# Values' product of weights as half-precision pairs, split in place among nine tiles of gates, and weight scales summed over partitions by TensorE

## The reference, cut to what matters

```
x = x + 0.5 * ffn(layernorm(x)); x = x + attn(layernorm(x)); x = x + 0.5 * ffn(layernorm(x))
# ffn(x): thought = x_norm[:, -1] @ agg_w, then four steps of thought += gelu(ln(thought) @ d1_w) @ d2_w
#         broadcast = thought @ bc_w;  gate = sigmoid(x @ gate_w);  out = layer_norm(x + gate * broadcast)
# attn(x): windows of 128, scores of own and previous window, squared relu, weighted sum of values
qkv = x @ w_attn.T          # q, k, v
sim = einsum('bwie,bwje->bwij', bq, bk2);  attn = square(relu(sim))
out = einsum('bwij,bwje->bwie', attn, bv2) @ w_o.T
```

## Time and profile before

| | us |
|---|---|
| runs of the kernel before: median (lowest to highest of 3) | 2115.79 (2107.5 to 2125.19) |
| the profiled execution's own time | 2117.86 |
| its span, first to last instruction | 2116.6 |
| PE busy in the span | 2037.7 (96%) |
| DVE / ACT / POOL busy | 1173.0 / 664.7 / 159.0 |
| DMA engines' mean share | 75.5%, 263 GB/s |

### The profile page before, as it was taken

One profiled execution on the slowest core, in us unless ns is written; L12 is line 12 of the kernel. 1 busy time (PEld: TensorE's weight loads), 2 busy tenths in 40 slices (PEclk: granted clock), 3 DMA queues, 4 the chain that ended last, 5 costly groups with the idle time before them and its releaser, 6 DMA issues.

```text
span 2116.6 us, 30247 instructions
## 1 busy us (share of the span) xinstructions
PE 2037.7 (96%) x11872; PEld 1037.0 (49%) x11872; DVE 1173.0 (55%) x2108; ACT 664.7 (31%) x931; POOL 159.0 (8%) x281
## 2 busy tenths in 40 slices
PE   8988989999999999998999999999999999999997
PEld 3333433444333446655665555665556564444443
DVE  2321323554344465567676755655555545888887
ACT  0557322433223232222333221211212113444443
POOL 0000000000000010000000000000000000111111
PEclk9999999999999999999999999999999999999999
DMA  8788897988988833348989799898987947555552
GB/s 340 237 311 341 285 353 269 379 319 320 354 338 333 332 132 118 100 140 299 323 294 327 273 320 293 297 347 283 313 290 278 357 149 221 149 151 154 154 149 80
DMA packets 275213, 555.76 MB, mean 263 GB/s; under 512 B 149040, under 2 KB 149248, under 8 KB 274688
## 3 DMA queue, kind: packets, MB, share of 16 engines
q1 hardware_dynamic: 275072, 553.83, 75.5%
HBM read 406.93 MB, written 113.26 MB: 246 GB/s over the span
## 4 chain that ended last, share of the span: by engine, by line
PE 47%; DMA 3%; DVE 2%; SPq 2%; ACT 1%; issue 1%; POOL 0%; ACTq 0%; DVEq 0%
PE product_banks L1023 41%; PE product_banks L1143 3%; PE thought_acc L1208 3%; DMA thought_units<-parts_scratch 1%; DMA gate_arena<-arena 1%; DMA arena<-in_x 0%; SPq L810 0%; DVE thought_units L1754 0%; SPq L944 0%; DMA thought_units<-in_d_w 0%; ACT arena L1315 0%; PE thought_turn L1216 0%; ACT arena L1318 0%; PE thought_acc L1198 0%; DVE arena L1566 0%
## 5 line engine op out<-in xcount | busy, mean ns | idle before, releaser
L1023 PE MATMUL product_banks<-gate_arena,arena 128*128 128x512 f16 x1536 | 354.1, 382 | 0.0
L1023 PE MATMUL product_banks<-wide_a,thought_units 128*128 128x512 f16 x1536 | 331.7, 379 | 0.0
L1023 PE MATMUL product_banks<-gate_arena,wide_a 128*128 128x256 f16 x2688 | 307.5, 274 | 2.4 <-DMA gate_arena<-arena 2.4
L1023 PE MATMUL product_banks<-wide_b,gate_arena 128*128 128x512 f16 x1344 | 301.8, 380 | 0.0
L1023 PEld LDWEIGHTS product_banks<-gate_arena,wide_a 128*128 128x128 f16 x2688 | 260.4, 98 | 59.5 <-issue 28.9
L1054 PE MATMUL product_banks<-wide_a,wide_b 128*128 128x512 f32 x512 | 240.9, 616 | 7.1 <-DMA wide_a<-in_w_attn 6.3
L1023 PEld LDWEIGHTS product_banks<-gate_arena,arena 128*128 128x128 f16 x1536 | 145.0, 98 | 203.6 <-issue 51.0
L1023 PEld LDWEIGHTS product_banks<-wide_a,thought_units 128*128 128x128 f16 x1536 | 150.3, 98 | 181.6 <-DVE arena L1606 0.5
L1023 PEld LDWEIGHTS product_banks<-wide_b,gate_arena 128*128 128x128 f16 x1344 | 127.2, 98 | 167.5 <-issue 24.9
L1423 DVE BATCH_NORM_STATS2 bn_parts<-arena 128x6 f32<-128x512 f32 x256 | 164.3, 684 | 4.4
L1054 PEld LDWEIGHTS product_banks<-wide_a,wide_b 128*128 128x128 f32 x512 | 95.1, 195 | 137.9 <-issue 137.8
(11 more groups left out here) (168 smaller groups left out, 2090.1 us busy)
## 6 DMA issues: line engine op xcount, KB each, us to landing
thought_units<-parts_scratch SPq DMA_DIRECT2D x268, 512.0 KB, 6.1
thought_units<-in_d_w SPq DMA_DIRECT2D x148, 512.0 KB, 6.7
thought_row<-in_d_w SPq DMA_DIRECT2D x76, 512.0 KB, 7.2
arena<-in_x SPq DMA_DIRECT2D x64, 512.0 KB, 8.8
parts_scratch<-thought_units SPq DMA_DIRECT2D x64, 512.0 KB, 6.2
x_scratch<-arena SPq DMA_DIRECT2D x64, 512.0 KB, 6.8
arena<-x_scratch SPq DMA_DIRECT2D x40, 512.0 KB, 6.0
gate_scratch<-arena SPq DMA_DIRECT2D x32, 512.0 KB, 8.3
```

The lines of the kernel that those rows point to most:

```text
L1023: mm = pe.matmul(bank, left(i, k), right(j, k), start=(n == 0), stop=(n == 3 * KD - 1))
```

## The change

- The fold `vo` becomes three f16 products for each float32 one. wv (in `wide_b`) and the transposed w_o (in `wide_a`) are split in place: the two halves of row block e are written over block e - 1, block 0's into a spare slot. So ACT's high half of block e waits for DVE's low half of e - 1 (`fold_split`). Before that, DVE takes the largest value of each block (`top`, 16 reductions of 128x1024) and two more scales are made (`wv`, `wo`). ACT's copy of the result is scaled by their inverse.
- The scale of a matrix: DVE reduces over the rows (`scale_t`), TensorE multiplies one column by a matrix that holds 1/1024 everywhere (`scale_a`, into a bank of the transposes), DVE multiplies by 1024 (`scale_b`). It is the sum over partitions of their largest values, where GpSimd's was the largest. There are now five scales.
- Nine tiles of gates stand before the fold `vo` (`EARLY` = 9): four with the loads of wv and w_o, five with the tops and splits. 19 tiles stand after it in place of 25, and they take the whole of reading back and splitting, and `gate_save`, which stood among the fold.
- The planner's cost of a `vo` piece goes from 1.83 to 1.28.
- In the first list the norms of the first two tiles stand before their transposes. In the first group of stage 2 the values of tile 0 come before the queries, and only these need the first transposed tile alone.

```diff
-EARLY, LATE = 3, 4
+EARLY, LATE = 9, 4
-        return 1.0 if piece[1:3] == ("qk", 0) else 1.83 * FOLD_SIZES[piece[2]]
+        return 1.0 if piece[1:3] == ("qk", 0) else (1.83 if piece[1] == "qk" else 1.28) * FOLD_SIZES[piece[2]]
...
+            own = [p for p in products if p[0] == "v" and p[2] == 0]
+            products = own + [p for p in products if p not in own]
...
-    early = paced([p for n in range(EARLY) for p in plan_gate(n)], wo, 0.9, PE_PIECES)
-    save = [("gate_save", k) for k in range(KD)] + [("params",)] + [("rest",)] * 6 + [("half_params",)]
-    fold_vo = paced(plan_fold("vo"), save, 0.5, PE_PIECES)
-    fold_vo.append(("fold_store", "vo", KD - 1))
+        if n >= 2:
+            wo.append(("top", "wv", n - 2))
+    wo += [("top", "wv", KD - 2), ("top", "wv", KD - 1), ("scale_t", "wv"), ("rest",), ("scale_a", "wv"), ("rest",),
+           ("scale_b", "wv")]
+    sides = [("top", "wo", e) for e in range(KD)] + [("fold_split", "wv", e) for e in range(2)] + [("scale_t", "wo")]
+    sides += [("fold_split", "wv", 2), ("scale_a", "wo"), ("fold_split", "wv", 3), ("scale_b", "wo")]
+    sides += [("fold_split", "wv", e) for e in range(4, KD)] + [("fold_split", "wo", e) for e in range(KD)]
+    early = paced([p for n in range(4) for p in plan_gate(n)], wo, 1.45, PE_PIECES)
+    early += paced([p for n in range(4, EARLY) for p in plan_gate(n)], sides, 0.75, PE_PIECES)
+    fold_vo = plan_fold("vo") + [("fold_store", "vo", KD - 1)]
...
-    gates = paced([p for n in range(EARLY, TILES - LATE) for p in plan_gate(n)], splits, 0.3, PE_PIECES)
+    gates = paced([p for n in range(EARLY, TILES - LATE) for p in plan_gate(n)], splits, 0.65, PE_PIECES)
...
+                        pe.wait_ge(side_split["wv"], e + 1)
+                        pe.wait_ge(side_split["wo"], e + 1)
...
+                        for n, (i, j) in enumerate(((0, 0), (0, 1), (1, 0))):
+                            mm = pe.matmul(bank_ap(key), fold_parts("wv", e)[:, i, d * P:(d + 1) * P],
+                                           fold_parts("wo", e)[:, j, h * BANK:(h + 1) * BANK], start=(e == n == 0),
+                                           stop=(e == KD - 1 and n == PARTS - 1))
...
+                pe.wait_ge(top_found, SCALE_AT[m] + 1)
+                pe.matmul(turn_ap((kind, m))[:, 0:1], mean_maker[:, :], scale_stat[m][:, KD:KD + 1], start=True,
+                          stop=True).then_inc(turn_full, 1)
...
+            elif kind == "fold_split":
+                m, e = a
+                if e == 0:
+                    act.wait_ge(scale_made, SCALE_AT[m] + 1)
+                else:
+                    act.wait_ge(side_split[m], e)
+                act.activation(fold_parts(m, e)[:, 0], fold_side[m][:, e, :], ACT.Copy,
+                               scale=scale_stat[m][:, KD + 2:KD + 3]).then_inc(side_high[m], 1)
...
+                if m == "wv":
+                    dve.wait_ge(q_piece[k], 32)
...
-                pool.partition_all_reduce(scale_stat[m][:, KD + 1:KD + 2], scale_stat[m][:, KD:KD + 1], P,
-                                          bass.bass_isa.ReduceOp.max).then_inc(top_shared, 1)
```

97 lines of the change are left out of this document (67 added, 30 removed).

## The result

The changed kernel takes 2137.39 us (median of 7 runs, 2130.0 to 2144.08), the kernel before 2115.02 (7 runs): 1.0102 of it, 95% interval 1.0073 to 1.0131. The forecast was 2089, faster. The profiled execution of the changed kernel spans 2139.3 us against 2116.6.

What follows compares the result with a forecast made beforehand. TensorE, busy 96% of the span, was taken to bound the kernel with its work and waits. 2117.9 - 26.9 - 28.9 + 10 + 12 + 5 = 2089.1 us, range 2064 to 2118.

Steps and rivals of the forecast that it cites:

- (a): Fold vo: 384 f16 products at 0.216 us replace 256 f32 instructions at 0.429 us, 82.9 for 109.8 us: -26.9 us.
- (c): Behind the fold: shorter heavy beats ask the DMA for 432 GB/s against 392 moved: +10 us, bounds 0 to 35.
- (b): Up to stage 2: four waits of TensorE leave with the lower clock behind them: -28.9 us, bounds -19.2 to -28.9.
- (d): Tiles ahead of the fold: chain of splits makes TensorE wait, DVE's 75 us against 70: +12 us, bounds 0 to 20.
- (e): One-column products for the scales: TensorE, in order, now waits for DVE: +5 us, bounds 0 to 12.
- The wait for the thought's sums: In the fold: TensorE's 6.34 us wait, put down to late stores, leaves with the lower clock behind it: -8.5 us.
- The wait before the first transposes: First tile: TensorE's 5.01 us wait for ACT's half of the norm leaves as norms come first: -5.0 us.
- the values first: Start of stage 2: 48 value products ahead remove the first queries' 4.07 us wait and slower run: -6.8 us.
- the fold's block e = 7: In the fold: its last split block, wanted some 18 us after the start, is one place where TensorE waits.
- the thought's split blocks: Ahead of the fold: TensorE waits for splits in the thought's t_unit, with only about 3.4 us of products ahead.
- late splits: Rival, tiles ahead of the fold: split links wait for other DVE work; at 8.2 us each, 2141 us; chance 0.06.
- wv's column: Scale of wv: its last load lands late, so TensorE waits 3.4 us ahead of the one-column product.

Runs made afterwards that it cites:

- f16 fold without the sides: The changed kernel without largest values, splits and scales of wv and w_o, its fold multiplying the split gate weights: 2095.12 us, 0.9902 of the kernel before.
- hand-offs apart: The changed kernel with a tile's moments two thirds of a half tile ahead of its norm, sigmoids one third behind gate results: 2107.30 us, 0.9968 of the kernel before.
- the two spares, GpSimd's scales and the three rows together: The changed kernel with two spare slots per factor, moments ahead of norms, sigmoids behind results, scales by GpSimd, three slots for the thought's split blocks: 2101.09 us, 0.9914.

## Why the prediction was wrong, point by point

By ratios the change falls into three steps: kernel before to f32 fold with the rest of the change, +0.0023; to the f16 fold without the sides, -0.0121; to the change, +0.0200. The +0.0023 takes in what was moved to make the waits leave, and the columns of three scales, so that the steps are near the terms and not the same. In us, beside the terms of the prediction:

| term | forecast | measured |
|---|---|---|
| (a) fold's products and (c) DMA | -26.9 + 10 = -16.9 | -25.6 |
| (b) waits that leave (measured: with all that was moved) | -28.9 | +5 |
| (d) splits and (e) scales | +12 + 5 = +17 | +42 |
| sum | -28.8 | +21.6 |

**(a)** was right. In the changed kernel 336 of the 384 products stand in one group, 76.5 us, 0.228 each, so some 87 us for all, where the two folds took 240.9 and the f32 fold alone that is left takes 121.9:

```profile
L1080 PE MATMUL product_banks<-wide_a,wide_b 128*128 128x512 f32 x256 | 121.9, 616 | 6.1 <-DMA wide_a<-in_w_attn 6.1
L1084 PE MATMUL product_banks<-wide_a,wide_b 128*128 128x512 f16 x336 | 76.5, 381 | 0.0
```

**(c)** was too high. Without the sides the waits for the thought's blocks up to stage 2 (11.9 and 4.1 us, and under 3 in smaller rows) are no more than 2 us above those with the f32 fold; behind the fold alone they are 14.2 us for 10.0. In stretches of 20 us the changed kernel's DMA moved up to 414 GB/s. The Trainium skill ("DMA: Bandwidth & Descriptors", Specifications) gives 358 GB/s as one core's limit towards memory; by it the heavy beats would have been held to the old pace, and the trace again does not bear it out.

**(b)** is the step that failed most: -28.9 was forecast, and +5 came of it together with the moves. I took each wait for the one hindrance at its place, and counted its whole length as won. Three things stood against it. The wait for the thought's sums (6.34 us in the earlier trace rows) I gave to the stores; ahead of the fold, with none of its stores near, it was 7.7 us in the f32 run and 9.3 without the sides. DVE's copy of the sums stands in order there behind the tokens' and the thought's low halves, and in the f32 run DVE idled 6.8 us for the tokens' high half, before which ACT had waited 2.0 and 1.3 us for the thought's rows. With the hand-offs apart it stays at 6.3 and 8.4 us in these two runs, so their order is not its main cause, and what makes it stays open. The wait before the first transposes (5.01 us) shrank to 0.71, but 2.8 us for the thought's blocks came 13 us later, and the four tiles with the loads idle 18.7 us where three had idled 17.7. And what was moved out of the fold and the early tiles stands among fewer tiles behind it, where PE idles 20.8 us for 11.0. Only the values first held, at 5 us for 6.8, since the scores wait for more now.

**(d)** failed in its sum and its wait. It had the right place and the right work (75 us of DVE; 73.3 in the trace), and the wrong rule. I compared DVE's work alone with TensorE's 70 us, and each link of the fold's own chain with 4.2 us. ACT's own 51.4 us I set against nothing. But ACT and DVE stood for each other at gate results, norms and splits all through that stretch (88.6 us of such waits in the rows above), so that it took nearly the sum of both, 124.7 us, against TensorE's 82.7. The runs with the hand-offs apart put some 19 of the sides' 42 us down to this order; the two spares, GpSimd's scales and the three rows together took about 11 more, and the last 11 stay open. And I named the wrong consumers: TensorE stood not for the fold's block e = 7, for which there were 18 us of cover, but for the two transpose banks and the four product banks, which DVE frees in the same queue (its wait for the thought's split blocks, which I had named too, was 1.7 us). The fold begins with all four product banks, so its start waited for the last gate result. My rival *late splits* had this sign and nearly the time (2141), but by luck: it needed links of 8 us, and the 16 low halves of the fold start from 281.91 to 349.48 us, 4.5 a link, near the 4.2 that I had.

**(e)** was near for wv's column (3.4 forecast, 5.04 measured), and too small for w_o's: that column waited 13.56 us for a bank; its largest values were known at 286.95 us (L1540), some 8 us before it ran. With GpSimd in its place the time was the same.

## What to carry to other kernels

When work is added to two in-order engines that hand results to each other, compare the sum of their work with the cover too, and not the larger alone, unless the list keeps each hand-off at least one item apart; a busy share of 64% on DVE and 45% on ACT was here nearly a full pair. A bank that is freed by a late engine can make TensorE wait before the data does. And a wait that is to be removed is worth its length only if nothing else is late behind it: the run with everything but the costly part would have shown at once that four such waits, with what was moved for their sake, were worth nothing together.

## What was not expected of the hardware

The lower clock behind the long waits costs some us more. Behind the wait of 13.6 us 24 products took 6.67 us, where 24 take 5.35 at full clock. Behind the wait of 15.0 us the fold's first 12 took 5.28 us, where 12 take 2.76 later in the same fold; the granted clock from 353.6 to 358.9 us is 0.50, the lower of the two levels (1.2 GHz). In the five tiles it is 0.86 in the mean, and 0.90 in the same stretch with the hand-offs apart.

What stays open: what makes up the 11 us that the sides still cost, what makes TensorE wait for the thought's sums in most versions, and why the values first add nothing once the order is mended.
